# A six-layer decoder kernel: another order of the steps of layer 2, and the gated layer's middle scores computed as blocks

## The chip, the cores and the metric

The kernel runs on one core of a Trainium2 chip. The metric is the device time of one execution in microseconds (us), the median of several runs. Instructions are issued by five engines, each in its own order: PE (TensorE, matmuls; its weight loads are shown as PEld), DVE (VectorE), ACT (ScalarE), POOL (GpSimd) and SP (SyncE, DMA issues). They meet only at semaphores.

## The reference

Six layers of a decoder, each followed by `x = layernorm(x + layer(x))`. `x` is 2 x 512 rows of 128 (eight tiles of 128 rows; "half 0" is the first sequence, tiles 0 to 3, "half 1" the second, tiles 4 to 7). The two layers that the change touches:

```python
# layer 2: attention to the context gives c_t, c_t modulates a state space model (S4D), then feed-forward
scores = einsum('bthd,bghd->bhtg', Q, K) / sqrt(DH)          # 4 heads, 77 context rows
topv, topi = top_k(scores, 32); attn = scatter(softmax(topv)) # the rest is zero
c_t = einsum('btg,bgd->btd', attn.mean(heads), V)
x = layernorm(x_text) * (1 + gate * scale_in(c_t)) + gate * shift_in(c_t)
y = irfft(rfft(x) * rfft(K_ssm)) + x * D_skip                 # convolution along the sequence
y = y * (1 + gate * scale_out(c_t)) + gate * shift_out(c_t)
xt = x_text + y
xt = xt + gelu(layernorm(xt) @ W1 + b1) @ W2 + b2
return layernorm(xt)

# layer 4: gated recurrence over time, 8 heads of 64
S = a_t[..., None] * S + k_t[:, None, :, None] * v_t[..., None, :]
o_t = einsum('bhcv,bhc->bhv', S, q_t)
```

Layer 1 is linear attention, layer 3 attention with 16 experts' projections, layer 5 cross attention with 16 heads, layer 6 a mixture of 16 experts.

## The kernel before

Layers 1 to 3 form one block, `first_layers`. It writes out for each engine the order of its steps: `one[...]` are steps of layer 1, `two[...]` of layer 2, `three[...]` of layer 3. Layer 2's steps are defined in `cross_attention_ssm`, one function per engine. An engine that waits holds everything behind it in its order.

In layer 2 each of the eight tiles g goes through: PE `score(g)` (L1099, L1100); ACT `scores(g)` copies it (L1221); DVE `select(g)` finds the 32 largest by four rounds of max and match-replace (L1371, L1374); POOL `shift(g)` subtracts the largest (L1301); ACT `exp(g)` (L1239); POOL `weigh(g)` masks (L1308, L1309; for tile 7 DVE does it, L1399); DVE `invert(g)` sums and takes the reciprocal (L1387); POOL `average(g)` forms the mean over heads (L1315 to L1318; for tiles 6 and 7 DVE does it, L1406 to L1408). The tiles' working buffers are two, by g % 2.

Per half b then follow: PE `mean(b)` turns the four means, with "unread" matmuls of the identity ahead of the last one (L1142, L1132), ACT copies, PE `c` (L1150), ACT copies, PE `film(b)` (L1157, one bank per tile); DVE `film(b)` adds the constants (L1414); `scale(b)` modulates the normed input (half 0 on POOL, L1325 and L1326; half 1 on DVE, L1423); POOL `affine(b)` (L1291, L1292) precedes it and `skip(b)` (L1331, L1334) follows it. PE `forth(b)` transforms (L1168, 64 instructions); DVE `multiply(b)` and `combine(b)` (L1440 to L1448) multiply with the kernel's transform; PE `back(b)` transforms back (L1181); DVE `modulate(b)` (L1457 to L1462) and `norm_ff(b)`; PE `up(b)` (transposes L1191, matmuls L1199), ACT `gelu(b)` (L1254), PE `down(b)` (L1209); DVE `leave(b)` (L1473), `move(b)`, `finish(b)`. DVE's `lower_weights` and `squares`, POOL's `split` and PE's `size` prepare layer 3.

PE's order from `forth(0)` on is the list `TAIL`, which also gives the bank of each result; the eight PSUM banks are handed on by use counts (`Ring`). film(0)'s four results share two banks (6 and 7), so that its third and fourth matmul wait until DVE has drained the first and second; film(1)'s last result goes to the bank of forth(0)'s real part.

In the gated layer (`gated_attention`, layer 4) a tile of 128 rows is cut in blocks of 32 (`BLK`, `NB` = 4). PE's `mid(g)` forms scores of keys against queries for the eight heads, two banks of four: first a full 128 x 128 product per head (L2608), then other products over the blocks above the diagonal (L2614, L2621), since those need other scalings; then it turns the keys (L2632). DVE's `mid(g)` copies the scores under a causal mask (L2957), so that what lies below the diagonal is never read. PE's order is back(g), mid(g+1), then projections of later tiles, then last(g) (L2671).

## Time and profile before

| | us |
|---|---|
| median of 3 runs | 580.77 (578.59 to 582.2) |
| the profiled execution | 581.28 |
| its span, first to last instruction | 579.5 |
| PE busy | 479.7 (83%) |
| DVE busy | 420.3 (73%) |
| ACT busy | 275.5 (48%) |
| POOL busy | 251.8 (43%) |
| mean granted TensorE clock | 0.889 |

Times in all views are us from the span's start. Layer 2 runs from about 87 to 210, layer 4 from 311 to 411. Busy time is that of all instructions of an engine; a "granted clock" of 1.00 is 2.4 GHz and 0.50 is 1.2 GHz.

### The profile page before, as it was taken

To read this page: it belongs to the slowest core of one execution; us is meant where nothing else is said; L and a number is where in the kernel's file an instruction comes from. 1 tells how busy PE (TensorE), PEld (TensorE's weight loads), DVE (VectorE), ACT (ScalarE), POOL (GpSimd) and SP (SyncE) were. 2 spreads that over 40 slices of the span, in tenths; PEclk is the share of its full clock that TensorE was granted. 3 is DMA by queue.
4 is the path that set the end of the run, shared out by engine and by line. 5 is a ranking of instruction groups with operands and counts; after the bars stand their busy time and mean duration, and the time that the engine had idled before them with its cause. 6 is when DMAs were issued, how large, how long until landed. Compare 5 with 4: busy or idle time off the path is not lost. (4 is left out here: it accounts for less than half of the span.)

```text
span 579.5 us, 12270 instructions
## 1 busy us (share of the span) xinstructions
PE 479.7 (83%) x4292; PEld 369.4 (64%) x4292; DVE 420.3 (73%) x1404; ACT 275.5 (48%) x673; POOL 251.8 (43%) x293
## 2 busy tenths in 40 slices
PE   3888792799599596799898999997999889689993
PEld 1565452486469564677593668775578645289983
DVE  4689949778997846865788999995697647237743
ACT  4599770430322245355412867562253413457741
POOL 3632499467902103355202443250577135516650
PEclk9978785589799885799999899979998979969998
DMA  8300004320000005706200000000472300251113
GB/s 250 121 2 1 1 2 148 89 94 2 2 0 1 2 26 135 130 1 111 40 1 0 1 2 2 1 2 2 183 314 67 88 0 34 60 144 48 47 48 103
DMA packets 27998, 33.39 MB, mean 58 GB/s; under 512 B 4961, under 2 KB 21073, under 8 KB 27426
## 3 DMA queue, kind: packets, MB, share of 16 engines
q1 hardware_dynamic: 26002, 29.13, 17.6%
q0 software_dynamic: 1504, 3.15, 1.6%
q8 instruction: 35, 0.57, 0.4%
q10 hardware_dynamic: 432, 0.33, 0.2%
q14 instruction: 25, 0.20, 0.1%
HBM read 26.44 MB, written 6.16 MB: 56 GB/s over the span
## 5 line engine op out<-in xcount | busy, mean ns | idle before, releaser
L2156 POOL TENSOR_TENSOR ea_scaled_rows<-ea_scaled_rows 128x768 f32<-128x768 f32 (+2 forms) x21 | 24.0, 1143 | 50.2 <-ACT ea_scaled_rows L2070 49.1
L3792 POOL DMA_INDIRECT em_results<-em_y_slot,slot_rows x31 | 29.7, 958 | 28.8 <-DVE em_y_slot L3919 28.2
L294 ACT ACTIVATE norm_log<-norm_var 128x4 f32<-128x4 f32 x20 | 4.1, 204 | 70.5 <-DVE norm_var L275 70.3
L3651 PE MATMUL banks<-em_slotT,em_weights 128*128 128x128 f32 x248 | 35.3, 288 | 2.6 <-ACT em_weights L3540 2.6
L3910 DVE SCALAR_TENSOR_TENSOR em_innerT<-banks,em_bias_of,em_soft 128x128 f32<-128x128 f32 x62 | 18.9, 346 | 22.7 <-ACT em_soft L3734 20.2
L38 PE MATMUL banks<-ea_w_high,ea_x_high 128*128 128x384 f32 x64 | 27.4, 428 | 8.6 <-DVE ea_acc L2247 8.5
L3651 PEld LDWEIGHTS banks<-em_slotT,em_weights 128*128 128x128 f32 x248 | 32.4, 204 | 3.3 <-issue 3.3
L2070 ACT ACTIVATE ea_scaled_rows<-banks,ea_gate 128x192 f32<-128x192 f32 x64 | 23.3, 418 | 18.7 <-PE banks L38 18.4
L2849 POOL TENSOR_TENSOR ga_sums<-ga_sums 128x512 f32<-128x512 f32 x8 | 9.1, 1136 | 42.8 <-DVE ga_sums L2910 42.8
L3734 ACT ACTIVATE em_soft<-banks,em_bias_of 128x128 f32<-128x128 f32 x62 | 19.4, 364 | 12.1 <-PE banks L3651 11.6
L38 PE MATMUL banks<-ea_w_low,ea_x_high 128*128 128x384 f32 x64 | 23.9, 373 | 0.0
L38 PE MATMUL banks<-ea_w_high,ea_x_low 128*128 128x384 f32 x64 | 23.7, 370 | 0.0
L654 POOL TENSOR_TENSOR lin_q_strip<-lin_qT,lin_strip_head 128x512 f32<-128x512 f32 x8 | 10.4, 1312 | 26.2 <-PE banks L544 16.9
L3787 POOL DMA_INDIRECT em_slots<-em_sent,em_where x16 | 15.7, 983 | 13.9 <-DVE em_where L3861 9.3
L3305 POOL TENSOR_TENSOR ca_prob<-ca_prob,ca_most 128x1232 f32<-128x1232 f32 x8 | 18.0, 2250 | 8.0 <-DVE ca_most L3360 8.0
L2243 DVE SCALAR_TENSOR_TENSOR ea_acc<-banks,ea_gate,ea_acc 128x192 f32<-128x192 f32 x24 | 10.0, 417 | 15.3 <-PE banks L38 15.0
L38 PEld LDWEIGHTS banks<-ea_w_high,ea_x_high 128*128 128x128 f32 x64 | 13.7, 215 | 10.9 <-DVE ea_acc L2247 9.6
L1374 DVE MATCH_REPLACE8 xa_left<-xa_top,xa_left 128x77 f32<-128x77 f32 x96 | 20.3, 222 | 0.0
L1181 PE MATMUL banks<-xa_part,cos_half 128*128 128x128 f32 x64 | 14.0, 305 | 7.1 <-DVE xa_part L1448 7.1
L3663 PE MATMUL banks<-em_down,em_innerT 128*128 x124 | 18.9, 276 | 0.6 <-DVE em_innerT L3910 0.6
L688 DVE TENSOR_TENSOR lin_scores<-banks,causal 128x2048 f32<-128x2048 f32 x8 | 18.2, 2270 | 0.0
L3247 ACT ACTIVATE ca_prob<-ca_prob 128x1232 f32<-128x1232 f32 x8 | 9.9, 1233 | 16.8 <-POOL ca_prob L3305 16.8
(521 smaller groups left out, 1539.4 us busy)
## 6 DMA issues: line engine op xcount, KB each, us to landing
em_up<-in_em_up SPq DMA_DIRECT2D x3, 1536.0 KB, 12.1
ea_wide<-ea_gates SPq DMA_DIRECT2D x4, 1024.0 KB, 11.8
em_down<-in_em_down SPq DMA_DIRECT2D x3, 768.0 KB, 13.7
em_slots<-slot_rows SPq DMA_DIRECT2D x1, 2108.0 KB, 10.4
w_qkv<-in_w_qkv SPq DMA_DIRECT2D x1, 1536.0 KB, 7.3
slot_rows<-em_slots SPq DMA_DIRECT2D x1, 1360.0 KB, 8.5
cos_half<-in_cos_half SPq DMA_DIRECT2D x1, 1024.0 KB, 7.3
sin_half<-in_sin_half SPq DMA_DIRECT2D x1, 1024.0 KB, 9.5
```

The source lines that it names most:

```text
L38: ins = pe.matmul(out, weights[w], data[d], start=(start and n == 0), stop=(stop and n == 2), **kw)
L688: dve.tensor_tensor(scores[:, g % 2].rearrange("p r j t -> p (r j) t"), scored.rearrange("p r j t -> p (r j) t"), spread(causal[:, :], 1, ...
L1374: ins = dve.match_replace(left[:, k, hh], top[:, k, r, hh], src[:, k, hh], SELECTED)
L2070: ins = act.activation(scaled_rows[:, g % 2, j - 1 + n], s.ps[:, n * QKV:(n + 1) * QKV], ACT.Copy, scale=gate[:, g, e:e + 1])
L2156: step(pool.tensor_tensor(scaled_rows[:, k, 0:n], scaled_rows[:, k, 0:n], scaled_rows[:, k, n:2 * n], ALU.add))
L3305: pool.tensor_tensor(p, p, spread(most[:, g % AHEAD], 2, [P, H, G]), ALU.subtract).then_inc(shifted, 1)
L3651: ins = pe.matmul(s.ps[:, k * P:(k + 1) * P], weights[:, n % NW, k // 2, k % 2 * P:(k % 2 + 1) * P], slotT[:, n], start=True, stop=True, s ...
L3663: ins = pe.matmul(s.ps[:, 0:P], innerT[:, n % NW, j], down_all[:, bass.ds(e, 1), j, :], start=(j == 0), stop=(j == 1))
L3734: act.activation(soft[:, n % NW, j], s.ps[:, j * P:(j + 1) * P], ACT.Silu, bias=bias_of[:, j, n:n + 1]).then_inc(soft_ready, 1)
L3787: pool.indirect_dma_start(core.slots[:, :], bass.IndirectOffsetOnAxis(ap=where[:, k, i:i + 1], axis=0), sent[:, i, k, :], None).then_inc(c ...
L3792: pool.indirect_dma_start(core.results[:, :], bass.IndirectOffsetOnAxis(ap=slot_rows[:, s, P:P + 1].bitcast(U32), axis=0), y_slot[:, s % N ...
L3910: dve.scalar_tensor_tensor(innerT[:, n % NW, j], s.ps[:, HE + j * P:HE + (j + 1) * P], bias_of[:, 2 + j, n:n + 1], soft[:, n % NW, j], ALU ...
```

## The change

It changes the order of layer 2's steps on PE (`TAIL`), POOL and DVE, and one loop of the gated layer. On PE, mean(1) and film(1) go ahead of back(0), and back(0) and forth(1) ahead of up(0). On DVE, select(5) goes ahead of film(0); multiply(0) and combine(0) go behind average(7), and film(1), scale(1), squares and lower_weights ahead of modulate(0) and norm_ff(0). On POOL, average(2) and average(3) follow weigh(3), ahead of affine(0); weigh(5) goes ahead of scale(0) and average(4), skip(0) ahead of shift(6), shift(7) behind affine(1) and two splits. DVE's average gets a wait for the means before it. In the gated layer the full product per head becomes its four diagonal blocks of 32 x 32.

```diff
--- before.py
+++ after.py
@@ -961,8 +961,8 @@
         sp.wait_ge(self.taps_in, 16)
 
 
-TAIL = [("forth", 0, (3, 4)), ("back", 0, (5,)), ("mean", 1, (6,)), ("film", 1, (0, 1, 2, 7, 3)), ("up", 0, (4, 5, 6, 0, 1)),
-        ("size", 0, (6,)), ("forth", 1, (2, 7)), ("down", 0, (3,)), ("back", 1, (4,)), ("turn", 0, (5,)), ("logit", 0, (6,)),
+TAIL = [("forth", 0, (3, 4)), ("mean", 1, (6,)), ("film", 1, (0, 1, 2, 7, 3)), ("back", 0, (5,)), ("forth", 1, (2, 7)),
+        ("up", 0, (4, 5, 6, 0, 1)), ("size", 0, (6,)), ("down", 0, (3,)), ("back", 1, (4,)), ("turn", 0, (5,)), ("logit", 0, (6,)),
         ("up", 1, (7, 4, 5, 6, 7)), ("down", 1, (4,))]
 
 
@@ -1402,6 +1402,8 @@
         def average(g):
 
             k = g % 2
+            if g == LAST_AVERAGES:
+                dve.wait_ge(mean_ready, g)
             dve.wait_ge(total_ready, g + 1)
             step(dve.tensor_tensor(prob[:, k], prob[:, k], spread(total[:, k], 2, [P, H, G]), ALU.mult))
             step(dve.tensor_tensor(prob[:, k, 0:2], prob[:, k, 0:2], prob[:, k, 2:4], ALU.add))
@@ -1684,28 +1686,30 @@
             kernel.near_product(pool, step)
             kernel.far_product(pool)
             two["shift"](0)
-            for g in range(NT):
-                if g < NT - 1:
-                    two["weigh"](g)
-                if g == 3:
+            for g in range(HT):
+                two["weigh"](g)
+                if g == HT - 1:
+                    two["average"](HT - 2)
+                    two["average"](HT - 1)
                     two["affine"](0)
-                elif g == HT:
-                    for b in range(B):
-                        two["bias"](b)
-                    two["scale"](0)
-                elif g == HT + 1:
-                    two["affine"](1)
-                elif g == NT - 2:
-                    for n in range(2):
-                        two["split"](n)
-                if g + 1 < NT and g + 1 != HT:
-                    two["shift"](g + 1)
-                if g < LAST_AVERAGES:
+                two["shift"](g + 1)
+                if g < HT - 2:
                     two["average"](g)
-                if g + 1 == HT:
-                    two["shift"](HT)
-                elif g == HT:
-                    two["skip"](0)
+            two["bias"](0)
+            two["weigh"](HT)
+            two["bias"](1)
+            two["shift"](HT + 1)
+            two["weigh"](HT + 1)
+            two["scale"](0)
+            two["average"](HT)
+            two["skip"](0)
+            two["shift"](HT + 2)
+            two["weigh"](HT + 2)
+            two["average"](HT + 1)
+            two["affine"](1)
+            for n in range(2):
+                two["split"](n)
+            two["shift"](HT + 3)
             two["split"](2)
             two["skip"](1)
             for b in range(B):
@@ -1758,26 +1762,26 @@
             two["norm_in"](1)
             two["invert"](3)
             two["select"](4)
+            two["select"](5)
             two["film"](0)
-            two["select"](5)
             two["invert"](4)
             two["select"](6)
             two["invert"](5)
-            two["multiply"](0)
-            two["combine"](0)
             two["select"](7)
             two["invert"](6)
             two["average"](6)
             two["weigh"](7)
             two["invert"](7)
             two["average"](7)
+            two["multiply"](0)
+            two["combine"](0)
+            two["film"](1)
+            two["scale"](1)
+            three["squares"]()
+            for n in range(4):
+                three["lower_weights"](n)
             two["modulate"](0)
             two["norm_ff"](0)
-            three["squares"]()
-            two["film"](1)
-            two["scale"](1)
-            for n in range(4):
-                three["lower_weights"](n)
             two["multiply"](1)
             two["combine"](1)
             three["sizes"]()
@@ -2604,9 +2608,12 @@
                     pe.wait_ge(products, products_before(g) + 2)
                     ks, qs = keys(k), queries(k)
                     for p in range(NP):
-                        for n in range(2):
-                            pe.matmul(both[n].ps[:, p * P:(p + 1) * P], ks[own(n), K_MID, p], qs[own(n), Q_MID, p],
-                                      start=True, stop=True, skip_group_check=True)
+                        for e in range(NB):
+                            for n in range(2):
+                                some = slice(e * BLK, (e + 1) * BLK)
+                                at = both[n].ps[some, p * P + e * BLK:p * P + (e + 1) * BLK]
+                                pe.matmul(at, ks[own(n), K_MID, p, some], qs[own(n), Q_MID, p, some], start=True,
+                                          stop=True, skip_group_check=True)
                     for p in range(NP):
                         for e in (0, 2):
                             for n in range(2):
```

## Rows read from the trace of the kernel before

**Rows 1.** Busy time by stretches: length, then busy us (instructions) per engine, clock, DMA.
```profile
128.80:163.50 34.70, 26.45 (x166) 21.73 (x165) 30.13 (x172) 6.64 (x16) 25.14 (x29) 0.90 0.00 1
163.50:186.80 23.30, 22.50 (x144) 17.18 (x142) 18.39 (x42) 7.37 (x12) 4.25 (x3) 1.00 0.00 1
...
343.00:370.00 27.00, 26.30 (x384) 21.32 (x382) 26.32 (x48) 18.95 (x41) 10.33 (x18) 1.00 0.01 2
```

**Rows 2.** Timeline of DVE, layer 2: start, duration, instruction, [idle before, releaser].
```profile
122.50 0.47 DVE L1387 TENSOR_REDUCE xa_total<-xa_prob 128x4 f32<-128x308 f32 x1 [1.09 <-POOL xa_prob L1309]
...
131.42 1.52 DVE L1414 SCALAR_TENSOR_TENSOR xa_film<-banks,rows,xa_film_const 128x512 f32<-128x512 f32 x2 [2.69 <-PE banks L1157]
...
134.92 0.65 DVE L1371 MAX8 xa_top<-xa_score 128x8 f32<-128x77 f32 x4
...
140.48 0.46 DVE L1387 TENSOR_REDUCE xa_total<-xa_prob 128x4 f32<-128x308 f32 x1
...
160.96 0.47 DVE L1399 SCALAR_TENSOR_TENSOR xa_prob<-xa_left,xa_prob 128x308 f32<-128x308 f32 x1
...
163.47 0.69 DVE L1457 TENSOR_TENSOR xa_xt<-banks,xa_xt 128x512 f32<-128x512 f32 x1
...
186.78 0.69 DVE L1473 TENSOR_TENSOR xa_xt<-banks,xa_u 128x512 f32<-128x512 f32 x1 [0.38 <-PE banks L1209]
```

**Rows 3.** Timeline of POOL, layer 2.
```profile
135.26 1.27 POOL L1325 TENSOR_TENSOR xa_u<-xa_u,xa_film 128x512 f32<-128x512 f32 x1 [0.69 <-DVE xa_film L1414]
...
141.33 0.30 POOL L1315 TENSOR_SCALAR xa_total<-xa_total,xa_text_weight 128x4 f32<-128x4 f32 x1
...
154.93 2.50 POOL L32 TENSOR_TENSOR ea_w_low<-w_qkv,ea_w_high 128x512 fp32r<-128x512 f32 x2
158.15 0.70 POOL L1301 TENSOR_TENSOR xa_prob<-xa_score,xa_top 128x308 f32<-128x308 f32 x1 [0.72 <-DVE xa_left L1374]
```

**Rows 4.** Timeline of PE, layer 2, behind the last average.
```profile
164.15 0.27 PE L1142 MATMUL banks<-ident,xa_mean 128*77 128x128 f32 x1
...
166.90 3.70 PE L1157 MATMUL banks<-xa_wfilm,xa_cT 128*128 128x512 f32 x8
...
171.71 3.70 PE L1199 MATMUL banks<-xa_hT,xa_w_scaled 128*128 128x512 f32 x8 [0.68 <-ACT xa_hT L1221]
...
175.77 3.82 PE L1168 MATMUL banks<-xa_u,cos_half 128*128 128x128 f32 x32
...
183.00 3.74 PE L1209 MATMUL banks<-xa_w,far 128*128 128x128 f32 x32
```

**Rows 5.** Timeline of ACT, layer 2: score(6)'s copy, the four gelus.
```profile
135.53 0.42 ACT L1221 COPY xa_score<-banks 128x308 f32<-128x308 f32 x1 [5.05 <-PE banks L1100]
...
174.21 2.42 ACT L1254 ACTIVATE far<-banks,xa_b_moved 128x512 f32<-128x512 f32 x4
```

**Rows 6.** Timeline of PE, gated layer, mid(7); weights 64*128 or 64*32, then data.
```profile
397.01 1.16 PE L2608 MATMUL banks<-ga_faded 64*128 64x128 f32 x16
398.10 0.46 PE L2614 MATMUL banks<-ga_faded 64*32 64x32 f32 x32
398.37 0.67 PE L2621 MATMUL banks<-ga_faded 64*32 64x64 f32 x32
```

**Rows 7.** Timeline of ACT, gated layer, behind mid(6).
```profile
392.45 0.59 ACT L2765 COPY ga_k_rows<-banks 128x512 f32<-128x512 f32 x1 [2.68 <-PE banks L2632]
```

**Rows 8.** DVE's waits from 343 to 410: releaser, us in total, times, longest.
```profile
DVE ga_res L2982 <- PE banks L2671: 6.5, 2, 3.8
...
DVE ga_scores L2957 <- PE banks L2621: 0.2, 1, 0.2
```

**Rows 9.** Busy time by stretches around PE's low clocks, columns as above.
```profile
144.00:152.40 8.40, 1.35 (x13) 1.16 (x11) 7.47 (x32) 2.00 (x6) 8.08 (x10) 0.89 0.00 0
152.40:157.30 4.90, 4.87 (x23) 4.87 (x24) 4.88 (x42) 2.06 (x5) 4.74 (x6) 0.50 0.01 2
...
379.00:386.60 7.60, 7.58 (x102) 6.87 (x100) 7.13 (x15) 3.87 (x12) 3.02 (x4) 0.55 0.01 2
```

## Prediction

> **What bounds the kernel now.** The sum below is made against the profiled run's own time, 581.28 us. The chain of work that ended last covers only the last 110 us, all behind the change, so it says nothing on either edited place. I therefore took busy time by stretches first [rows 1]. In layer 2, from film(0) to the last average, DVE works 30.1 of 34.7 us; from there to leave(0) PE works 22.5 of 23.3 us. In the middle of the gated layer DVE works 26.3 of 27.0 us and PE 26.3: both are full, and only a wait can tell which one leads. Then I read the timelines of DVE, POOL, PE and ACT through layer 2 [rows 2 to 5], and of PE and ACT at the end of the gated layer with DVE's waits there [rows 6 to 8]. What follows leave(0), DVE's first step behind down(0), keeps its order, and each layer needs the one before, so I take a shift of leave(0) as a shift of the end.
>
> **Layer 2 up to the last average.** In before DVE waits 1.09 us in front of invert(3) for POOL's weigh(3), and 2.69 us in front of film(0) for PE [rows 2]. The change puts POOL's weigh(3) ahead of average(2), so invert(3) starts when DVE is free, at 122.50 - 1.09 = 121.41, and select(4) ends at 131.42 - 2.69 - 1.09 = 127.64. Then select(5) goes ahead of film(0): 134.92 to 140.48 is 5.56 us, so it ends at 133.2, and the wait for PE is covered. So far a gain. Its film takes as long as from 131.42 to 134.92, 3.5 us: until 136.7.
>
> But two of film(0)'s four matmuls need a bank that DVE drains, and score(6) stands behind them on PE. From DVE's first film operation to the end of ACT's copy of score(6) it took 135.53 + 0.42 - 131.42 = 4.53 us before [rows 2, 5]; after, the copy ends at 137.7, and exp(5), behind it on ACT, at about 138.2. POOL's weigh(5) waits for that, and behind it in POOL's order now stand scale(0), average(4), skip(0), shift(6), weigh(6), average(5), affine(1), two splits and only then shift(7). Before, POOL did the same without scale(0) and shift(7), and without a gap, from 141.33 to 154.93 + 2.50 = 157.43: 16.1 us [rows 3]. Add scale(0), two operations of 1.27 us (2.6), shift(7) 0.7, and 0.55 for exp(6), a round trip to ACT that average(5) covered before: 19.95 us. average(5) ran beside DVE's combine(0) then and will not, which I estimate at 0.7 us less: 19.25. So shift(7) ends at 157.4 and exp(7) between 157.9 and 158.6.
>
> DVE is ready earlier: select(6) from 137.75, invert(5), select(7), each select 5.6 us: 149.5. It then waits for weigh(6), average(5) and shift(7). From weigh(7) to the end of average(7) is 163.47 - 160.96 = 2.51 us [rows 2]. So average(7) ends between 160.4 and 161.1; I take 160.6, which is 2.9 us before the 163.47 of now. forth(0), which now starts some 5 us later (scale(0) is behind weigh(5)), ends near 150 to 153 and delays nobody, since multiply(0) moved behind average(7).
>
> **From the last average to leave(0).** Before, PE had done back(0) by then, under DVE's select(7). After, PE does everything in a row: mean(1), film(1), back(0), forth(1), up(0), down(0). The terms [rows 4, 5]: from the mean's last transpose to film(1) 166.90 - 164.15 = 2.75; film(1) with the transposes and the copy ahead of up(0) 171.71 - 166.90 = 4.81; forth(1), 64 instructions, 183.00 - 175.77 = 7.23; back(0), 64 instructions of the same shape, 7.23; up(0) with ACT's table load and four gelus, which forth(1) covered before, 174.21 + 2.42 - 171.71 = 4.92; down(0) until leave(0) 186.78 - 183.00 = 3.78. Sum 30.7 us, so leave(0) at 191.3 against 186.78: 4.5 us later. DVE's own work fits beside it: multiply(0) and combine(0) end before film(1) has filled its banks, and scale(1), lower_weights, modulate(0) and norm_ff(0) lie beside back(0) and forth(1). The balance: 2.9 us won ahead of average(7), 7.4 us lost behind it.
>
> The clock comes on top. In before PE was nearly idle from 144 to 152.4, and the granted clock of the following 4.9 us was 0.50, that is 1.2 GHz instead of 2.4: they did the work of 2.45 us [rows 9]. After the change PE stands from the end of the mean's unread matmuls (about 156) until 160.6, with other gaps before. I take it that the next 4.9 us go at 1.2 GHz; some 1.2 us of them are ACT copies, so the loss is about 1.9 us. Bounds: nothing, and 3.2 us if it stays low for the 7.6 us that it stayed low at 379 [rows 9]. Layer 2 is 6.4 us slower, or 4.5 with a full clock.
>
> **The other edits of layer 2** cost nothing: average's added wait stands where DVE waits for shift(7) anyway; squares and lower_weights change place inside the cover of back(0); the bias operations run while POOL waits for exp(4) and select(5), the splits are in POOL's sum. The banks of each stage stay the same; film(1)'s last bank needs multiply(0), which DVE does first. No DMA moves.
>
> **The gated middle scores.** Each mid(g) now issues 16 PE instructions of 64x128 keys on 128 columns, 398.10 - 397.01 = 1.09 us; after, 64 of 64x32 on 32 columns. The next line runs just that shape: 32 in 398.37 - 398.10 = 0.27 us, 8.4 ns each, so 64 take 0.54: 0.55 us less of PE per mid, eight times [rows 6]. The other bound is the line after, 64 columns wide: 32 are busy 0.67 us, 21 ns each, 64 in 1.3 us, 0.25 us worse than now. I take the same shape.
>
> Little of these 4.4 us can reach the end: of DVE's waits behind 343, PE ends one of 0.2 us and two at the very end, 6.5 us together, the longer 3.8 and so the other 2.7 [rows 8]. That other one follows mid(7); and ahead of it ACT waits 2.68 us for PE behind mid(6), for the copy of its turned keys, ahead of the state blocks that back(6) needs [rows 7]. Two times 0.55 is 1.1; mid(5), at a low clock now, feeds the same chain, which I estimate at 0.4 more. Gain 1.5 us; bounds a loss of 0.5 and a gain of 2.2.
>
> By the Trainium skill, "TensorE: Matmul & The Clock Gate", section "Wait — 56ns, not 53.3ns?", the start-to-start of matmuls never drops under about 25 ns however few their columns. By that, 64 instructions would take 1.6 us, 0.5 us more than now, this edit would speak against itself, and the sum would be near 589.7. The trace does not agree here: 8.4 ns for instructions on alternating parts of the array.
>
> **The sum.** +6.4 - 1.5 = +4.9 us on the profiled run's 581.28: 586.2. The median of the three runs is 580.77, 0.5 us below it: 585.7.
>
> **The rivals.** (1) The clock stays full at film(1): 4.5 - 1.5, 583.8. For it: the mean's unread matmuls cut the gap. Against it: by my times PE would stand about 4 us three times between 138 and 160. (2) On the other side, not slower: POOL does not lead. If shift(7) came in time, DVE would end average(7) two rounds of 2.51 us after 149.5, at 154.5, and leave(0) would be 6.1 us earlier: 579.6, and 577.7 with a full clock. It decides from the point where POOL's 19.25 us shrink under 13.5; against it, most of them were gapless before. (3) The blocks do not overlap well in the array: 1.3 us a mid; two mids in the tail and the three between 343 and 370, where PE has no slack, cost 0.25 each, so 585.7 + 1.5 + 1.25 = 588.5. For it only that eight places of the array alternate where the row shows four. (4) PE in the gated layer now gets gaps in each step and falls to 1.2 GHz once more; at 379 it did so for 7.6 us [rows 9]; half of that, less DVE's slack, is about 2.5: 588.2. (5) The low clock at film(1) lasts 7.6 us: 587.0.
>
> **How the numbers follow.** Forecast 0.50, rival 1 0.19, rival 2 0.09, rival 3 0.04, rival 4 0.09, rival 5 0.09. The predicted time is 585.7. The range leaves out most of rival 2 below and the ends of rivals 3 and 4 above: 581.0 to 588.5. One per cent, about what this kernel's measurement can tell from no change, is 5.8 us: 575.0 to 586.6. Faster than that needs rival 2 and a further gain: 0.03. Slower: rivals 3 to 5 and a fifth of the forecast: 0.33. Within: 0.64.
>
> **What would show it.** In the profile after: select(5) ahead of film(0) without a wait of 2.7 us; POOL nearly without a gap from weigh(5) to shift(7), and a DVE wait of about 4 us in front of weigh(7); average(7) near 160.6; PE in a row from film(1) to down(0); DVE waits in front of sizes and leave(0), together 6 us or so; leave(0) between 191 and 193.5. In the gated layer 64 instructions in 0.54 us, and DVE's wait behind mid(7) ending 1 to 2 us earlier, measured from the layer's start. I am wrong if weigh(7) doesn't wait, if back(0) finds a gap ahead of average(7), or if leave(0) comes before 187.

## The result and the profile after

The changed kernel takes 593.61 us in the median (590.82 to 595.49, four runs) against 580.67 (578.59 to 582.2) for the one before: a ratio of 1.0229, 95% interval 1.0186 to 1.0273. A second series beside the last group of experiments gave 591.94 (587.11 to 596.57) and 1.0167, 1.0106 to 1.0228. Ratios are set against executions of the kernel before that were made beside each kernel, and leave out executions more than 1.5% above their kernel's fastest, so they are not quotients of the medians. Forecast was 585.7, with a range from 581.0 to 588.5. The changed kernel is slower, by about 10 to 13 us instead of 4.9.

The busy time of the engines is the old one; they only wait longer. The page's first two lines of after:

```profile
span 589.0 us, 13040 instructions
...
PE 479.0 (81%) x4676; PEld 366.7 (62%) x4676; DVE 421.7 (72%) x1404; ACT 275.1 (47%) x673; POOL 254.1 (43%) x293
```

Before it reads 579.5 us of span with PE 479.7, DVE 420.3. To place the 9.5 us of span, one must first know that the profiled executions don't enter layer 2 at the same moment. The first operation of DVE's second input norm, which the change does not touch, in before and then in after (start, duration, instruction):

```profile
118.37 0.86 DVE L270 BATCH_NORM_STATS2 norm_stats<-x 128x6 f32<-128x128 f32 x4
```

```profile
116.15 0.86 DVE L270 BATCH_NORM_STATS2 norm_stats<-x 128x6 f32<-128x128 f32 x4
```

After is 2.2 us ahead there by luck: in that execution PE's matmuls for the state space kernel, which the change does not touch, had 1.23 us of gaps without a releaser, and 3.47 us in before. So 2.2 has to be added to a time of after in layer 2 before it is held against the forecast.

DVE's timeline of after from film(0) to leave(0), against [rows 2]; behind the instruction stand, in brackets, the idle time ahead of it and its releaser:

```profile
131.56 1.39 DVE L1416 SCALAR_TENSOR_TENSOR xa_film<-banks,rows,xa_film_const 128x512 f32<-128x512 f32 x2
134.25 0.75 DVE L1416 SCALAR_TENSOR_TENSOR xa_film<-banks,rows,xa_film_const 128x512 f32<-128x512 f32 x1 [1.29 <-PE banks L1157]
135.95 0.75 DVE L1416 SCALAR_TENSOR_TENSOR xa_film<-banks,rows,xa_film_const 128x512 f32<-128x512 f32 x1 [0.96 <-PE banks L1157]
...
152.15 1.35 DVE L1408 TENSOR_TENSOR xa_prob<-xa_prob,xa_total 128x308 f32<-128x308 f32 x1 [0.94 <-POOL xa_mean L1318]
...
158.16 1.04 DVE L1399 SCALAR_TENSOR_TENSOR xa_prob<-xa_left,xa_prob 128x308 f32<-128x308 f32 x1 [2.32 <-ACT xa_prob L1239]
...
161.08 0.24 DVE L1410 TENSOR_TENSOR xa_mean<-xa_prob 128x77 f32<-128x77 f32 x1
...
193.60 0.69 DVE L1475 TENSOR_TENSOR xa_xt<-banks,xa_u 128x512 f32<-128x512 f32 x1 [1.90 <-PE banks L1209]
```

The wait of 2.69 us ahead of film(0) is gone, as forecast; two others stand inside film(0), and average(7) ends at 161.3 (163.5 with the 2.2). Before, its last operation stood in the same place:

```profile
163.32 0.24 DVE L1408 TENSOR_TENSOR xa_mean<-xa_prob 128x77 f32<-128x77 f32 x1
```

From the start of this operation to leave(0) it was 23.5 us, and is 32.5. PE's timeline of after, against [rows 4]:

```profile
127.27 1.98 PE L1157 MATMUL banks<-xa_wfilm,xa_cT 128*128 128x512 f32 x4
132.35 3.56 PE L1157 MATMUL banks<-xa_wfilm,xa_cT 128*128 128x512 f32 x4 [3.09 <-DVE xa_film L1416]
...
161.37 0.33 PE L1142 MATMUL banks<-ident,xa_mean 128*77 128x128 f32 x1 [2.09 <-DVE xa_mean L1410]
...
164.63 4.65 PE L1157 MATMUL banks<-xa_wfilm,xa_cT 128*128 128x512 f32 x8
169.12 0.38 PE L1181 MATMUL banks<-xa_part,cos_half 128*128 128x128 f32 x2
...
176.26 3.74 PE L1168 MATMUL banks<-xa_u,cos_half 128*128 128x128 f32 x32
...
183.41 0.60 PE L1191 MATMUL banks<-ident,xa_h 128*128 128x128 f32 x4
184.68 3.70 PE L1199 MATMUL banks<-xa_hT,xa_w_scaled 128*128 128x512 f32 x8 [0.68 <-ACT xa_hT L1221]
...
189.75 3.81 PE L1209 MATMUL banks<-xa_w,far 128*128 128x128 f32 x32 [0.85 <-ACT far L1254]
```

Film(0)'s second four instructions take 3.56 us where the first four take 1.98: PE waited 3.09 us for a bank and then ran at half clock (length, busy us of PE, PEld, DVE, ACT and POOL, clock 0.50, DMA):

```profile
132.60:136.00 3.40, 3.40 (x5) 1.33 (x5) 1.15 (x3) 0.00 (x0) 0.00 (x0) 0.50 0.00 0
```

Behind average(7) PE works in one row, mean, film(1), back(0), forth(1), up(0), down(0). Last, POOL, against [rows 3]: weigh(5), waiting 5.80 us for the exponential of the late score(6), then the last line ahead of shift(7), and shift(7) itself, with no gap between:

```profile
138.22 0.98 POOL L1308 TENSOR_SCALAR xa_left<-xa_left 128x308 f32<-128x308 f32 x1 [5.80 <-ACT xa_prob L1239]
...
154.41 2.56 POOL L32 TENSOR_TENSOR ea_w_low<-w_qkv,ea_w_high 128x512 fp32r<-128x512 f32 x2
156.93 0.70 POOL L1301 TENSOR_TENSOR xa_prob<-xa_score,xa_top 128x308 f32<-128x308 f32 x1
```

The gated layer, from PE's first matmul of its values to the start of DVE's last result, took 94.9 us before (first two rows) and 97.0 after (last two):

```profile
311.59 1.09 PE L2533 MATMUL banks<-ga_wo,ga_vcT 128*64 128x128 f32 x16 [0.48 <-PEq L1551]
406.51 0.29 DVE L2982 SCALAR_TENSOR_TENSOR ga_res<-x,banks 128x128 f32<-128x128 f32 x1 [3.75 <-PE banks L2671]
...
318.97 1.09 PE L2537 MATMUL banks<-ga_wo,ga_vcT 128*64 128x128 f32 x16 [0.48 <-PEq L1553]
416.02 0.29 DVE L2989 SCALAR_TENSOR_TENSOR ga_res<-x,banks 128x128 f32<-128x128 f32 x1 [3.75 <-PE banks L2678]
```

The blocks do what they should: their line, L2615, starts at 363.85, the next line, L2621, at 364.38.

```profile
363.85 0.72 PE L2615 MATMUL banks<-ga_faded 64*32 64x32 f32 x62
364.38 0.21 PE L2621 MATMUL banks<-ga_faded 64*32 64x32 f32 x1
```

That is the forecast 0.54 us for 64 instructions to within a hundredth, against 1.09 before [rows 6]. By the Trainium skill, "TensorE: Matmul & The Clock Gate", section "Wait — 56ns, not 53.3ns?", matmuls start no less than about 25 ns apart, so an estimate from that page would be 1.6 us; the trace disagrees with that here.

So in the profiled pair: 2.2 us of luck, nothing won ahead of the last average, 9.0 lost behind it, 0.6 between leave(0) and layer 4, 2.1 in the gated layer.

### The profile page after: what moved, and what is told of

Read it like the earlier page. It is cut to its first block and busy times, and to the rows that moved or that the text cites. A ratio compares the mean times of both kernels' runs of the same rounds, so it can differ in the third digit from the quotient of the medians.

```text
span 589.0 us, 13040 instructions
## 1 busy us (share of the span) xinstructions
PE 479.0 (81%) x4676; PEld 366.7 (62%) x4676; DVE 421.7 (72%) x1404; ACT 275.1 (47%) x673; POOL 254.1 (43%) x293
## 5 line engine op out<-in xcount | busy, mean ns | idle before, releaser
L3658 PE MATMUL banks<-em_slotT,em_weights 128*128 128x128 f32 x248 | 35.1, 288 | 2.6 <-ACT em_weights L3547 2.6
L3658 PEld LDWEIGHTS banks<-em_slotT,em_weights 128*128 128x128 f32 x248 | 32.3, 203 | 3.3 <-issue 3.3
L3741 ACT ACTIVATE em_soft<-banks,em_bias_of 128x128 f32<-128x128 f32 x62 | 19.4, 364 | 12.0 <-PE banks L3658 12.0
L654 POOL TENSOR_TENSOR lin_q_strip<-lin_qT,lin_strip_head 128x512 f32<-128x512 f32 x8 | 12.2, 1534 | 24.1 <-PE banks L544 14.9
L3670 PEld LDWEIGHTS banks<-em_down,em_innerT 128*128 128x128 f32 x124 | 16.3, 192 | 0.8 <-issue 0.8
```

Of the source, the lines that this page charges most:

```text
L3658: ins = pe.matmul(s.ps[:, k * P:(k + 1) * P], weights[:, n % NW, k // 2, k % 2 * P:(k % 2 + 1) * P], slotT[:, n], start=True, stop=True, s ...
L3670: ins = pe.matmul(s.ps[:, 0:P], innerT[:, n % NW, j], down_all[:, bass.ds(e, 1), j, :], start=(j == 0), stop=(j == 1))
L3741: act.activation(soft[:, n % NW, j], s.ps[:, j * P:(j + 1) * P], ACT.Silu, bias=bias_of[:, j, n:n + 1]).then_inc(soft_ready, 1)
```

## The experiments

Stage lengths, from the starts of the same instructions in each kernel's one profile (us). "Ahead" is from PE's first matmul behind the state space taps (103.66 in before, 101.44 in after) to the start of the last operation of average(7), "row" from there to leave(0), "gated" as above. That last operation takes 0.24 us, but 1.18 in shift_early and warm_shift, so by its end their "ahead" is 0.9 longer against the others, and their "row" 0.9 shorter. Of before and of each kernel:

| | median | ratio to before, interval | ahead | row | gated |
|---|---|---|---|---|---|
| before | 580.67 | | 59.7 | 23.5 | 94.9 |
| after | 593.61 | 1.0229 (1.0186 to 1.0273) | 59.6 | 32.5 | 97.0 |
| after_again | 591.94 | 1.0167 (1.0106 to 1.0228) | 57.9 | 32.5 | 97.0 |
| layer2_only | 595.06 | 1.0221 (1.0138 to 1.0303) | 59.7 | 33.6 | 96.3 |
| blocks_only | 580.68 | 0.9995 (0.9961 to 1.0029) | 59.0 | 23.0 | 96.9 |
| film0_only | 584.56 | 1.0068 (1.0029 to 1.0107) | 65.9 | 23.0 | 94.6 |
| half1_only | 587.51 | 1.0143 (1.0100 to 1.0186) | 57.2 | 32.5 | 94.7 |
| shift_early | 591.22 | 1.0189 (1.0138 to 1.0241) | 57.3 | 35.1 | 93.6 |
| back_early | 597.02 | 1.0278 (1.0227 to 1.0330) | 60.9 | 37.9 | 95.1 |
| keep_warm | 590.09 | 1.0163 (1.0117 to 1.0209) | | | |
| warm_shift | 589.01 | 1.0123 (1.0077 to 1.0169) | 55.5 | 32.1 | 98.2 |
| mid_double | 582.57 | 1.0046 (1.0013 to 1.0078) | 59.1 | 23.0 | 96.8 |
| full_filled | 581.66 | 1.0014 (0.9980 to 1.0048) | 59.0 | 23.0 | 96.3 |
| blocks_filled | 581.49 | 0.9969 (0.9934 to 1.0003) | 59.0 | 23.0 | 94.5 |

Of keep_warm no stage lengths are given; warm_shift has the same edit.

### Which part carries the loss

**layer2_only**: after, with before's full products in the gated layer.

> All of layer 2's new order, the gated layer as before. Theory A (the loss is mostly layer 2's serial PE chain from film(1) to down(0), the gated blocks add the rest): 8 to 10 us slower than before, 589 to 591, and in the profile leave(0) 30 to 33 us behind the end of average(7). Theory B (layer 2 is worth what the profile of the changed kernel shows at its face, 6.5 us, and the gated layer costs most of the other 6): 5 to 7 us slower. Theory C (the gated blocks carry the loss): under 4 us slower.

**blocks_only**: before, with the blocks alone (the diff's last hunk).

> Layer 2 as before, the gated middle scores as blocks. Theory A and B: the blocks do save 0.55 us of PE in each of the eight tiles, but the gaps that they leave let the granted clock fall more often, above all around mid(6), so the kernel is 2 to 5 us slower, 583 to 586; the profile then shows a second stretch at 0.5 to 0.65 within the gated layer. The rival is the prediction's own term: 1.5 us faster, 579, the fall in the changed kernel being chance.

Layer 2 carries the whole loss: 14 us in the median, about 13 by the ratio, where 8 to 10 were expected. The blocks change nothing in the median; neither the expected 2 to 5 us of loss nor a gain is seen, though the interval, from 2.3 us faster to 1.7 slower, leaves room for the predicted 1.5. And layer2_only's gated layer took 96.3 us although it has no blocks, so 97.0 can't be put down to the blocks as such.

**film0_only**: before, with POOL's new order, the added wait in DVE's average, and

```diff
             two["select"](4)
+            two["select"](5)
             two["film"](0)
-            two["select"](5)
```

> Only the reorder around half 0's film: POOL's new order, and select(5) ahead of film(0) on DVE; multiply(0), combine(0), the list of PE's tail and the gated layer as before. Theory A: it wins nothing and loses little, 1 us faster to 2 us slower (580 to 583), because film(0)'s third and fourth matmul wait for DVE and score(6) for them; back(0) still lies ahead of average(7). Rival D (the late weigh(5) on POOL is what costs): 5 us slower or more.

**half1_only**: before, with the new `TAIL` and DVE's new order from select(7) on, and the added wait in its average; POOL and film(0) as before.

> Only half 1's film and transforms ahead of half 0's inverse and feed-forward (PE's tail list, DVE's order from select(7) on); POOL's order and film(0) as before, the gated layer as before. Theory A: this carries layer 2's loss, 6 to 8 us slower (587 to 589): average(7) ends about 2.4 us earlier than before, but leave(0) 30 to 33 us behind it instead of 23. Rival D: 3 us slower or less.

The two halves of the change lose in different places. In half1_only the last average comes 2.5 us sooner, because multiply(0) and combine(0) have left, and the row is 9.0 longer: 6.6 together; the medians say 6.5 (580.99 for before beside it), the ratio 8.3. film0_only is 3.9 us slower by the ratio, more than theory A's 2 and less than rival D's 5. Its row is as before, and the loss lies ahead of the average (6.3 us in the profiled execution, which at 588.01 us was 3.4 above its median), in multiply(0), whose two waits on DVE were not there before:

```profile
150.65 0.69 DVE L1442 TENSOR_TENSOR xa_part<-banks,kernel_re 128x512 f32<-128x512 f32 x1 [4.88 <-PE banks L1168]
154.12 0.69 DVE L1442 TENSOR_TENSOR xa_part<-banks,kernel_im 128x512 f32<-128x512 f32 x1 [2.19 <-PE banks L1168]
```

scale(0) now stands behind weigh(5) on POOL, so forth(0) is late. The full change moves multiply(0) away from this wait, but half1_only, without any edit at film(0), has its last average sooner (57.2) than the full change (59.6 and 57.9), and the lower median. So the reorder around film(0) buys nothing.

### What holds the last average, and what the row is made of

**shift_early**: after, with

```diff
             two["average"](HT + 1)
+            two["shift"](HT + 3)
             two["affine"](1)
             for n in range(2):
                 two["split"](n)
-            two["shift"](HT + 3)
```

> The changed kernel with POOL's shift(7) ahead of affine(1) and the two splits. Theory A (POOL leads the last average, as predicted): in after POOL had no gap from weigh(5) at 138.22 to shift(7) at 156.93, and DVE waited 0.94 us ahead of average(6) and 2.32 ahead of weigh(7). Shift(7) now comes up to 4.8 us sooner, the second wait goes and average(6)'s operations, 1.1 to 1.35 us each beside POOL's splits, shrink too: last average and leave(0) 2.3 to 3.5 us sooner, median 590 to 591.5. Theory B (DVE leads; its own operations slow down beside POOL's whichever of them these are): the wait goes, but weigh(7) and average(7) now run beside affine(1) and the splits and take longer; under 1 us of gain, 592.5 to 594.

By the table the average came 2.4 us sooner than in after, but by the end of its last operation only 1.4; the median lies inside the spread of after. So both theories are seen in part. The wait ahead of weigh(7) is gone, but now average(7) runs beside the splits. DVE in shift_early:

```profile
158.24 1.49 DVE L1408 TENSOR_TENSOR xa_prob<-xa_prob,xa_total 128x308 f32<-128x308 f32 x1
159.76 1.26 DVE L1409 TENSOR_TENSOR xa_prob<-xa_prob 128x154 f32<-128x154 f32 x1
161.06 1.18 DVE L1410 TENSOR_TENSOR xa_mean<-xa_prob 128x77 f32<-128x77 f32 x1
```

3.93 us for what took 1.04 in after (0.48, 0.32 and 0.24), where POOL had less beside it. Average(6) and weigh(7), which had stood beside POOL's work in after, got back 2.0 us, so 0.9 of the 2.3 us of wait that went was lost again. From the start of average(6) to the end of average(7) it is 7.7 us instead of 9.2. In this execution film(1) ran at half clock for longer (5.36 us for its 8, 4.65 in after), which made the row 35.1, or 33.9 from the end of the average.

**keep_warm**: after, with unread matmuls in PE's waits:

```diff
 mean_of(b):
-                if i == HT - 1:
+                if b == 1 and i >= 2:
+                    ring[f"c{b}"].claim(pe)
+                    short_unread(ring[f"c{b}"].ps, 14)
+                elif i == HT - 1:
 film_of(b):
+                if b == 0 and g == 2:
+                    ring["xr0"].claim(pe)
+                    short_unread(ring["xr0"].ps, 14)
 forth(b):
+            if b == 0:
+                ring["xr0"].claim(pe)
+                short_unread(ring["xr0"].ps, 16)
```

> The changed kernel with more unread matmuls of the identity on PE, nothing else moved: 14 while film(0)'s third matmul waits for DVE (3.09 us in the profile of after), 16 ahead of forth(0), 14 instead of none ahead of mean(1)'s third transpose and 14 instead of 8 ahead of its last. They go into banks that the next step overwrites. Theory A (in these waits the granted clock falls, and film(0) and film(1) pay for it): in after, film(0)'s second half took 3.56 us for 4 instructions where the first half took 1.98, and film(1) 4.65 us for 8 where before had 3.70. With the waits filled film(0)'s four take about 2.0, score(6)'s copy and weigh(5) come 1.6 us sooner and so does the last average; film(1) with the copies around it gives back 1 to 1.5. Profile 2.5 to 3 us shorter between the taps and leave(0), median 588 to 591, and the high ones among the runs of after (mean clock 0.880 to 0.885) go, so that the spread shrinks. Theory B (the clock is a companion, the order is the cost): POOL's sequence from weigh(5) on and the row on PE are as long as before, 592 to 595.

**warm_shift**: keep_warm and shift_early together.

> The two remedies together in the changed kernel: the unread matmuls on PE in film(0)'s and mean(1)'s waits, and POOL's shift(7) ahead of affine(1) and the splits. Theory A (film(0) at 1.2 GHz and POOL's sequence each hold the last average back, one after the other, so they add): the last average 3.5 to 4.5 us sooner than in after, measured from the state space columns (55.2 to 56.2 us instead of 59.7), the row behind it unchanged at 32 to 33; median 586.5 to 589. Theory B (both move the same wait): last average 2 to 2.5 us sooner, 589.5 to 591.5. Either way it stays 5 us or more behind the kernel before, since PE's row from film(1) to down(0) is untouched: 23.5 us there before, 32.4 after.

**after_again**: after, once more.

> The changed kernel once more, beside the others of this group, for a firmer median and a second profile. Theory A (the loss is the order of layer 2, about 9 to 10 us, and the rest is where PE's clock happens to fall): median 591 to 595, layer 2 from the state space columns to leave(0) again 91 to 94 us, the gated layer anywhere from 93.5 to 97 with its low clocks in other places than before. Theory B (the gated layer's 97.0 belongs to the blocks): low clocks at 32 to 40 and 76 to 84 us from its first value again, 96.5 to 97.5.

In warm_shift film(0)'s wait is filled and its second part runs at full clock (1.98 us for its four instructions):

```profile
131.91 3.29 PE L1132 MATMUL banks<-xa_w,ident 128*128 128x128 f32 x28
135.16 1.98 PE L1163 MATMUL banks<-xa_wfilm,xa_cT 128*128 128x512 f32 x4
```

But after_again did so without any filling, behind nearly the same wait:

```profile
132.92 1.98 PE L1157 MATMUL banks<-xa_wfilm,xa_cT 128*128 128x512 f32 x4 [2.72 <-DVE xa_film L1416]
```

and its last average came 1.7 us sooner than after's. It is the exception: after, layer2_only, film0_only, shift_early and back_early, the other profiles with this order and without filling, all fell to half clock there, behind waits of 2.89 to 3.10 us, and needed 2.50 to 3.56 us for the four instructions. Counted from the first matmul behind the taps, POOL's weigh(5) starts at 36.7 to 36.9 us in these five, and at 35.1 in after_again and in warm_shift. After_again's row, and warm_shift's:

```profile
137.09 0.98 POOL L1308 TENSOR_SCALAR xa_left<-xa_left 128x308 f32<-128x308 f32 x1 [4.10 <-ACT xa_prob L1239]
```

```profile
139.33 0.98 POOL L1317 TENSOR_SCALAR xa_left<-xa_left 128x308 f32<-128x308 f32 x1 [4.10 <-ACT xa_prob L1248]
```

So the half clock at film(0) is worth 1.7 us, and most executions that were profiled have it. In warm_shift the last average starts its last operation at 55.5, as theory A said; by its end it is 3.2 us sooner than in after, 1.7 from film(0) and 1.5 from shift(7): the two add up. The clock was up behind the average too:

```profile
161.00:192.00 31.00, 29.34 (x201) 24.00 (x202) 21.51 (x47) 7.37 (x12) 4.14 (x3) 1.00 0.00 1
```

From the end of the average to leave(0) warm_shift needs 30.9 us, after 32.3: the low clock there is worth 1.4. In time little of this can be told from noise. keep_warm's ratio is that of after_again, and its spread, 586.6 to 595.7, did not shrink as theory A had it. warm_shift has the lowest ratio of this group, clear of the first series of after but not of after_again. The change stays about 7 us behind the kernel before, as both theories had it.

**back_early**: after, with

```diff
-TAIL = [("forth", 0, (3, 4)), ("mean", 1, (6,)), ("film", 1, (0, 1, 2, 7, 3)), ("back", 0, (5,)), ("forth", 1, (2, 7)),
+TAIL = [("forth", 0, (3, 4)), ("back", 0, (5,)), ("mean", 1, (6,)), ("film", 1, (0, 1, 2, 7, 3)), ("forth", 1, (2, 7)),
             two["average"](6)
+            two["multiply"](0)
+            two["combine"](0)
             two["weigh"](7)
             two["invert"](7)
             two["average"](7)
-            two["multiply"](0)
-            two["combine"](0)
```

> The changed kernel with multiply(0) and combine(0) on DVE between average(6) and weigh(7), and back(0) on PE ahead of mean(1): half 0's inverse transform is then taken out of the row that starts at the last average. Theory A (the row on PE is the loss, as predicted; back(0) is 7.2 us of it): DVE's 4.5 us of multiply and combine fill its 2.3 us of wait, so the last average comes 2 to 2.5 us later; from there to leave(0) 25 us instead of 32.4; sum 4.5 to 5.5 us less, median 588 to 589.5. Theory B (the row waits for something else: modulate, norm and gelus of half 0 would be late by themselves): less than 2 us, 591.5 to 594. Theory C (PE no longer idle ahead of mean(1) also keeps its clock): A and 1 to 2 us more, 586 to 588.

All three theories were wrong: nothing was gained, and the median lies 3.4 and 5.1 us above the two series of after (the interval overlaps that of the first). PE in back_early:

```profile
163.38 0.80 PE L1181 MATMUL banks<-xa_part,cos_half 128*128 128x128 f32 x2 [7.91 <-DVE xa_part L1450]
...
172.51 0.49 PE L1142 MATMUL banks<-ident,xa_mean 128*77 128x128 f32 x3
```

back(0) starts 2.6 us before average(7) is done (165.97) and, partly at half clock, holds mean(1) until 172.5. It did not leave the row, it went to its front, and scale(1), which it covered in after, is open now: PE stands 2.5 us ahead of forth(1). For back(0) to be out of the row it has to start at least its own 7 us ahead of the end of average(7); before, it started 11 us ahead, at 152.44. For that forth(0) and so scale(0) must be early. That is what the change gave up.

### The gated layer

**mid_double**: before, with each full product issued twice (`for p in [*range(NP), *range(NP)]`).

> The kernel before with the gated layer's full products of the middle scores issued twice, the second over the first: 1.09 us more of PE in each of the eight mids, twice what the blocks took away, with the other sign. Prediction's theory (PE sets the time of the last two mids and a little of mid(5): 0.55 us less gave 1.5): 1.09 more cost 2.5 to 4 us, 583.5 to 585. Theory B (PE has slack in every step but the last, and what the blocks save it only waits longer): 0 to 1.2 us, 581 to 582.2, and in the profile the gated layer from its first value to its last result takes 95 to 96 us. Theory C (PE has no slack from mid(3) to mid(5) either): 4 to 8 us, 585 to 589. If it costs little, the blocks could not have given anything, and their zero is explained without the clock.

8.7 us more of PE cost 2.7 us by the ratio, which is within the prediction's 2.5 to 4, and 1.9 in the median (580.64 for before beside it), between that and theory B. The gated layer took 1.9 us more, although its clock was never low, in 96.8 us (columns as above):

```profile
307.20:404.00 96.80, 87.25 (x1177) 67.19 (x1178) 82.64 (x173) 56.14 (x119) 33.61 (x52) 1.00 0.01 2
```

So PE's time in the mids does count, at 0.2 to 0.3 us per us in this pair, whose clocks differ. In the other kernels the clock falls in this layer, for 3 to 10 us at a time, and not in the same places. Before, then after, then shift_early, two stretches each; a clock of 0.57 means half clock in 6.8 of the 8 us:

```profile
327.60:335.60 8.00, 8.00 (x30) 5.26 (x32) 7.79 (x9) 5.30 (x12) 5.75 (x7) 0.57 0.01 2
375.60:387.60 12.00, 10.21 (x119) 8.56 (x117) 11.33 (x21) 7.21 (x15) 6.25 (x10) 0.72 0.01 1
```

```profile
351.00:359.00 8.00, 8.00 (x152) 6.09 (x153) 7.56 (x16) 3.35 (x9) 3.65 (x8) 0.57 0.01 2
395.00:403.00 8.00, 6.88 (x144) 4.70 (x144) 5.79 (x12) 2.54 (x6) 3.47 (x6) 0.57 0.02 5
```

```profile
336.80:344.80 8.00, 8.00 (x67) 5.30 (x69) 7.79 (x9) 5.30 (x12) 5.77 (x7) 0.57 0.01 2
384.80:392.80 8.00, 5.75 (x150) 4.55 (x149) 7.57 (x16) 5.06 (x11) 4.38 (x6) 0.79 0.01 2
```

Counted from each layer's first matmul the low clock begins at 16 and 68 us in before, at 32 and 76 in after, and at 16 and 68 in shift_early, which has the blocks and low clocks where before has them, the second 3.4 us shorter: its gated layer takes 93.6, 1.3 less than before. After_again is low at 32 and 76 once more and takes 97.0, and blocks_only too, with 96.9; so far theory B of after_again is right. Warm_shift, with the blocks, is low at 30, for 10 us, and at 78, and takes 98.2. But the blocks do not decide it: back_early, which has them, is low at 68 and 81 and takes 95.1, and layer2_only, with full products, is low at 32 and takes 96.3. Film0_only and half1_only, with full products, are low at 68 alone and take 94.6 and 94.7. So near 30 us the clock falls in four of the table's six profiles with blocks and in one of the four with full products, of those without filling or doubling in this layer; that the blocks' longer waits cause it is argued, not shown. What is seen in after is that at 76 it hits the tail. DVE's wait for PE in front of mid(6)'s copy, 0.2 us before [rows 8], reads in after (us in total, times, longest):

```profile
DVE ga_scores L2964 <- PE banks L2628: 1.6, 1, 1.6
```

**blocks_filled** (blocks_only) and **full_filled** (before) get unread matmuls in PE's waits of the gated layer:

```diff
 mid(g):
-                        unread(pe, both[0], ident[:, :], t["ga_wa"][:, :], 2)
+                        unread(pe, both[0], ident[:, :], t["ga_wa"][:, :], 3)
 back(g):
                     s.claim(pe)
+                    if g in (0, 4, 5, 6, 7):
+                        unread(pe, s, ident[:, :], t["ga_wa"][:, :], 1 if g > 5 else 2)
```

> The kernel before with the blocks, and with unread matmuls of 512 columns in PE's waits of the gated layer: one more ahead of mid(0), two ahead of back(0), back(4) and back(5), one ahead of back(6) and back(7), each shorter than the wait that it stands in. Theory A (the blocks' gain is eaten by low clocks that their idle time lets in): no low clock behind the first value, or one short one; gated layer 92.5 to 94 us where blocks_only took 96.9 and before 94.9; median 577.5 to 579.5. Theory B (the clock falls wherever it does, not because of these waits): 95 to 97, and 580 to 582.

> The kernel before with its full products and the same unread matmuls as blocks_filled: what is left between the two is the blocks alone, at one clock. Theory A (prediction's term: the blocks give 1 to 1.5 us where the clock is the same): gated layer 94 to 95 us, 1 to 1.5 more than blocks_filled, median 579 to 580.5. Theory B (the blocks give nothing): the same as blocks_filled within 0.5 us.

The second low clock is gone in both; the first stays, at 31 for 3.4 us in blocks_filled and at 16 for 6.8 us in full_filled, so the two are not at one clock either. Theory A's bounds for the layer were missed by 0.5 and 1.3 us, those for the median by 2.0 and 1.2. Nor did filling help as such: full_filled, with one low clock less than before, has a gated layer 1.4 us longer. Between the two filled kernels lie 1.9 us of gated layer and 0.45% of time, but the medians are 0.2 us apart and the intervals overlap: blocks_filled has five runs from 576.4 to 578.3 and seven from 580.8 to 583.4. It has the lowest ratio of all kernels here, with an interval that just reaches 1 and a median that is above that of before.

## Why the prediction was wrong

**What bounds the kernel, POOL's sequence: right.** From weigh(5) to the end of shift(7) 19.25 us were forecast, and it took 157.63 - 138.22 = 19.4; DVE waits for it ahead of average(6) and weigh(7), 3.3 us against about 4.

**Select(5) covers film(0)'s wait: right, and worth little.** DVE reached film(0) at 131.56, 133.8 with the 2.2, against 133.2. The 0.6 were lost ahead of it: two small operations of the input norm took 0.73 and 0.60 us instead of 0.26 and 0.16, and invert(3) started at 119.86 + 2.2 = 122.1 instead of 121.41.

**"Its film takes as long as from 131.42 to 134.92, 3.5 us": the first step that failed.** It took 5.1, with two waits for PE. I had copied the duration from an execution in which PE waited for DVE inside film(0) hardly at all. With DVE late by a select, PE's third matmul waits 3.09 us, and behind that wait ran at half clock. The wait alone does not lengthen the film: in after_again, with 2.72 us of it and a full clock, DVE's film(0) takes 3.6 us. The prediction had a low clock at film(1) and put it at nothing here; it measured 1.7 us. So score(6) and weigh(5) came 2.2 us later than forecast (138.22 + 2.2 against 138.2), 0.6 from ahead of film(0) and the rest from the clock, and the same 2.2 went through POOL's nearly gapless sequence to shift(7). Weigh(7), 1.04 us beside a split instead of 0.47, added most of the rest. Of the 2.9 us ahead of average(7) nothing was left in after. In after_again, with the clock up, 1.8 were.

**From the last average to leave(0): right.** 30.7 us and 1.9 for the clock were forecast, 32.6; it is 32.3 from the end of average(7). Term by term: last transpose to film(1) 3.26 (forecast 2.75), film(1) 4.49 and the transposes with their copy 1.27 (4.81 together), back(0) 7.14 and forth(1) 7.15 (7.23 each), up(0) to down(0) 5.07 (4.92), down(0) to leave(0) 3.85 (3.78). The extra of 1.5 us at the mean and film(1) is the low clock, forecast at 1.9. warm_shift, at full clock, took 30.9 against the 30.7, and half1_only shows the 9.0 us by themselves.

**The gated blocks, -1.5: the second step that failed.** Count and duration were right, and rival 3 (no overlap in the array) fell. But the sum took the low clocks of before as given, and in after, after_again and blocks_only they lie at 32 and 76 us instead, with a gated layer that is 2.0 to 2.1 us longer than before's. That comes near to rival 4, which had 0.09, though the clock fell elsewhere and not once more. That the blocks themselves save time is not shown: 1.3 us in shift_early and 1.9 between the filled pair are from single profiles, whose low clocks differ in length too. In the medians of ten runs of blocks_only nothing is left of the 1.5, to within 0.4%. How often the clock falls where, and why, stays open.

**The other rivals.** POOL did lead (against rival 2), the clock at film(1) was low in after (against 1) and not for longer than forecast (against 5).

**The sum.** 2.9 lost ahead of the average and 3.6 in the gated layer are 6.5 us on top of 4.9: 11.4. The profiled pair, with the 2.2 us of luck taken out, differs by 11.7; the rest is 0.6 between leave(0) and layer 4, less 0.3 in the row. The first series of medians differs by 12.9: the profiled execution of after, 590.82 us at a mean clock of 0.888, was the shortest of its four, and where the other three (593.1 to 595.5, at 0.880 to 0.885) lost more, no profile shows. By the medians the gated layer has no share in the loss, by the profiled pair it has 2.1 us; that is open as well. The range was too narrow because each row of the sum came from one execution, and those that hang on the clock differ by 2 us from one to the next. The sign of layer 2 was right, and the row behind the average was priced to 0.3 us.

Why the medians of layer2_only and of the two series of after, the same order in layer 2, lie up to 3 us apart is open. In half1_only's ten runs the clock goes with the time: six with a mean of 0.893 or more took 585.9 to 588.1 us, four at 0.890 or less 590.5 to 594.2; in which stage these four lost it no profile shows.

## What to carry to other kernels

A step that runs under the cover of another engine's long work costs nothing there; moved behind the last result of that work it stands in the row and costs all of itself, so count the row from the last input to the next barrier for each order before choosing one. When a consumer is made later, look at whoever waits for the buffers it drains, and at what that producer has queued behind. A duration taken from one profile holds for the waits and the clock of that profile: where the edit changes the waits ahead of a matmul, put its half-clock duration into the range.

## What the runs showed of the hardware

The same code does not meet the low clock in the same place each time: behind 3.09 us of wait film(0)'s four instructions took 3.56 us in after, behind 2.72 us 1.98 in after_again, and in the gated layer layer2_only is low at 32 us, half1_only, with the same code there, at 68. By the Trainium skill, "TensorE: Matmul & The Clock Gate", section "What's actually happening", the gate watches PE in a rhythm of its own that does not start with the kernel; these runs would fit that, but no run here shows the rhythm itself.

DVE's operations with two inputs in SBUF can take far longer beside POOL: a 128x308 product 1.35 and 1.49 us instead of 0.48, a 128x77 sum 1.18 instead of 0.24. In after the three operations of average(6) end at 153.50, 154.62 and 155.84, each 0.1 to 0.3 us behind the end of one of POOL's (153.16, 154.45 and 155.75). By the Trainium skill, "SBUF — State Buffer", section "Who interferes with whom", a DVE instruction with two SBUF inputs contends with a GpSimd instruction that reads SBUF; the trace agrees.
